# Small-head attention: value products in two runs of six chunks, and stationary operands padded to 128 columns

## The reference, cut to what matters

```python
# L0: 16 heads, head size 8, masked; L3: the same without bias and mask, scale 128 ** -0.5
qh = (q @ Wq.T + bq).reshape(B, 56, 16, 8).transpose(0, 2, 1, 3)      # B = 16
kh = (k @ Wk.T + bk).reshape(B, 1500, 16, 8).transpose(0, 2, 1, 3)
vh = (v @ Wv.T + bv).reshape(B, 1500, 16, 8).transpose(0, 2, 1, 3)
score = einsum('bhqd,bhkd->bhqk', qh, kh) / sqrt(8)
score = where(kv_mask[:, None, None, :], score, -10000.0)
attn = softmax(score, axis=-1)
out = einsum('bhqk,bhkd->bhqd', attn, vh)
return out.transpose(0, 2, 1, 3).reshape(B, 56, 128) @ Wo.T + bo
```

## Time and profile before

| what | value |
|---|---|
| runs, median (lowest, highest) | 2214.21 (2211.83, 2214.41) us |
| span of the profiled execution | 2210.2 us |
| busy in that span: PE, DVE, ACT, POOL | 93%, 67%, 54%, 34% |
| mean granted TensorE clock | 0.953 of 2.4 GHz |
| largest groups of L0: exp L654, reduction L798, product L511 | 198.1, 153.4, 133.5 us |

### The profile page before, as it was taken

The page is one execution under the profiler, slowest core; times in us unless marked ns, Lnnn a source line. Parts: engine busy times, 40 slices in busy tenths (PEclk is TensorE's granted clock), DMA queues, the critical chain, the costliest instruction groups (busy, mean ns, idle before and its releaser), DMA issues. The chain is left out here.

```text
span 2210.2 us, 47308 instructions
## 1 busy us (share of the span) xinstructions
PE 2062.2 (93%) x18797; PEld 1505.9 (68%) x18797; DVE 1482.6 (67%) x3068; ACT 1200.2 (54%) x2313; POOL 752.7 (34%) x337
## 2 busy tenths in 40 slices
PE   5999999866999899999999999999997799999996
PEld 3677777655887455677777777777764457777774
DVE  5677777688986554566666666666626577777774
ACT  5877887634766222344444444444421467777763
POOL 6565566016875470112111211112000254433410
PEclk8999999967999898999999999999997889999997
DMA  6554544233540311231112211131000354544420
GB/s 161 148 148 132 159 134 132 63 85 97 143 136 20 79 38 39 70 104 66 60 60 82 97 60 60 60 100 62 1 1 25 87 159 126 149 126 139 122 79 9
DMA packets 94541, 199.78 MB, mean 90 GB/s; under 512 B 42113, under 2 KB 50353, under 8 KB 94066
## 3 DMA queue, kind: packets, MB, share of 16 engines
q1 hardware_dynamic: 94322, 196.75, 30.3%
HBM read 116.22 MB, written 0.65 MB: 53 GB/s over the span
## 5 line engine op out<-in xcount | busy, mean ns | idle before, releaser
L1630 PEld LDWEIGHTS L2ps<-L2probsT,L2values 125*128 125x128 f32 (+1 forms) x2688 | 317.4, 192 | 51.3 <-issue 48.9
L1611 PE MATMUL L2ps<-L2keys,L2qz 128*128 128x501 f32 x672 | 340.2, 590 | 0.9 <-DVE L2out_bias L1847 0.9
L1630 PE MATMUL L2ps<-L2probsT,L2values 125*128 125x128 f32 (+1 forms) x2688 | 318.5, 275 | 0.5 <-ACT L2probsT L1740 0.5
L1725 POOL TENSOR_TENSOR L2keys<-L2keys,L2mean_spread 127x1500 f32<-127x1500 f32 x15 | 50.9, 3395 | 583.0 <-DMA L2wqk<-L_moments 583.0
L1823 DVE CUSTOM_DVE_ANT_0 L2work<-L2ps,L2maskadd,L2big 128x1503 f32<-128x1503 f32 x112 | 199.5, 1781 | 72.9 <-PE L2ps L1611 72.7
L1625 PEld LDWEIGHTS L2ps<-const,L2work 128*126 128x126 f32 x1344 | 164.3, 140 | 118.7 <-issue 116.5
L654 ACT ACTIVATE L3probsT<-L3ps 128x448 f32<-128x448 f32 x384 | 196.0, 547 | 71.1 <-PE L3ps L511 66.5
L654 ACT ACTIVATE L0probsT<-L0ps 128x448 f32<-128x448 f32 x384 | 198.1, 551 | 47.7 <-PE L0ps L511 46.6
L1625 PE MATMUL L2ps<-const,L2work 128*126 128x128 f32 x1344 | 202.8, 273 | 3.5 <-DVE L2work L1832 3.1
L1742 ACT COPY L2qz<-L2ps 128x128 f32<-128x128 f32 x112 | 29.7, 265 | 304.7 <-PE L2ps L1630 304.7
L798 DVE TENSOR_REDUCE L0partmax<-L0ps 112x1 f32<-112x1000 f32 x128 | 153.4, 1199 | 58.1 <-PE L0ps L484 56.0
(11 more groups left out here) (479 smaller groups left out, 4164.7 us busy)
## 6 DMA issues: line engine op xcount, KB each, us to landing
L0key_stack<-L0key_parts SPq DMA_DIRECT2D x192, 187.5 KB
L3key_stack<-L3key_parts SPq DMA_DIRECT2D x192, 187.5 KB
L0ctxT<-in_ctxT SPq DMA_DIRECT2D x16, 750.0 KB, 4.4
L1rawT<-in_ctxT SPq DMA_DIRECT2D x16, 750.0 KB, 6.5
L2raw<-in_ctx SPq DMA_DIRECT2D x16, 750.0 KB
L3ctxT<-in_ctxT SPq DMA_DIRECT2D x16, 750.0 KB, 4.4
L2mean_spread<-L_moments SPq DMA_DIRECT2D x15, 750.0 KB, 6.7
L2wqk<-L_moments SPq DMA_DIRECT2D x15, 750.0 KB, 8.4
```

The lines of the kernel that those rows point to most:

```text
L1611: last = nc.tensor.matmul(PS[:, 3 * (m % 2) + c, 0:NPR], tile_rows(m), KT[:, m // RT % 2, 500 * c:500 * c + NPR], start=True, stop=True)
L1630: last = nc.tensor.matmul(PS[:, bank, 0:P], V[0:keys_in(c), i // RT % 2, c, :], PT[0:keys_in(c), i % 2, c, :], start=c == 0, stop=c == NCH ...
```

## The change

- `values` is called at two steps of four, n % 4 == 1 and 3, and computes six chunks each time. The waits on `pv_done` and on the emptied S units are counted accordingly.
- QS gets 128 columns per pair, of which the last 16 are zero; `scores0` and `scores12` load all 128 as stationary columns and write all 128 partitions of banks 0 to 2. DVE still reads 112 partitions.
- HL becomes a view of HLW, which has 128 more columns of zeros; M loads 128 stationary columns, from the maxima of its pair on, and writes 128 partitions; ACT still reads the first 2 or 3.
- GpSimd sets the padding to zero at the start, with a semaphore `pads_set`, for which TensorE waits ahead of its loop and DVE ahead of the first `row_maxima`.

```diff
@@ attention_16_small_heads
+    RUNS = 2
+    RUN_STEPS = (1, 3)
...
-        QS = sb("query_stack", [ROWS, 4, 4, TT], BF16)
+        QS = sb("query_stack", [ROWS, 4, 4, P], BF16)
...
-        HL = sb("maxparts", [TT, 2, 4, 2 + NM], BF16)
+        HLW = sb("maxparts", [TT, 2, 4 * (2 + NM) + P], BF16)
+        HL = HLW[:, :, 0:4 * (2 + NM)].rearrange("p u (t n) -> p u t n", t=4)
...
-                    sp.dma_start(QS[n:16 * NC:NC, slot], QM[rows, part, b].rearrange("p j q -> p (j q)")
+                    sp.dma_start(QS[n:16 * NC:NC, slot, :, 0:TT], QM[rows, part, b].rearrange("p j q -> p (j q)")
...
-                nc.tensor.matmul(PS[0:TT, 0, 0:500], QS[0:SROWS, h % 4, tau, :], KS[0:SROWS, h % 4, tau, 0:500],
+                nc.tensor.matmul(PS[:, 0, 0:500], QS[0:SROWS, h % 4, tau, :], KS[0:SROWS, h % 4, tau, 0:500],
...
-                    last = nc.tensor.matmul(PS[0:TT, c, 0:500], QS[0:SROWS, h % 4, tau, :],
+                    last = nc.tensor.matmul(PS[:, c, 0:500], QS[0:SROWS, h % 4, tau, :],
...
             def values(h, part):
                 b, u = divmod(h, 2)
-                wait_emptied(pe, plan.emptied("S", 4 * h + 3, (3 * part + 2) // 4))
+                length = KC // RUNS
+                wait_emptied(pe, plan.emptied("S", 4 * h + 3, (length * (part + 1) - 1) // 4))
...
-                for c in range(3 * part, 3 * part + 3):
+                for c in range(length * part, length * (part + 1)):
...
-                                                QS[:, h % 4, tau, :], start=True, stop=True)
+                                                QS[:, h % 4, tau, 0:TT], start=True, stop=True)
...
-                        last = nc.tensor.matmul(PS[0:2 + NM, bank, tau * TT:(tau + 1) * TT], HL[:, i % 2, tau, :], IB[:],
+                        last = nc.tensor.matmul(PS[:, bank, tau * TT:(tau + 1) * TT], HLW[:, i % 2, tau * (2 + NM):tau * (2 + NM) + P], IB[:],
...
+            pe.wait_ge(s.pads_set, 2)
...
-                h, part = n // 4 - 1, n % 4
-                if 0 <= h < HB:
-                    values(h, part)
+                h = n // 4 - 1
+                if 0 <= h < HB and n % 4 in RUN_STEPS:
+                    values(h, RUN_STEPS.index(n % 4))
...
             nc.gpsimd.memset(MINUS[:], -1.0).then_inc(s.minus_set, 1)
             pool.wait_ge(s.minus_set, 1)
+            nc.gpsimd.memset(QS[:, :, :, TT:P], 0.0).then_inc(s.pads_set, 1)
+            nc.gpsimd.memset(HLW[:], 0.0).then_inc(s.pads_set, 1)
+            pool.wait_ge(s.pads_set, 2)
             if masked:
-                nc.gpsimd.memset(QS[96:97], 125.0).then_inc(s.q_rows_set, 1)
+                nc.gpsimd.memset(QS[96:97, :, :, 0:TT], 125.0).then_inc(s.q_rows_set, 1)
...
-                        act.wait_ge(s.pv_done, 4 * h - 4)
+                        act.wait_ge(s.pv_done, RUNS * (h - 1))
...
-                        act.wait_ge(s.pv_done, 8 * i - 8)
+                        act.wait_ge(s.pv_done, 2 * RUNS * (i - 1))
...
-                    ins = nc.scalar.copy(QS[96:ROWS, i % 4].rearrange("p t n -> p (t n)"), PS[0:2 + NM, bank, 0:HALF])
+                    ins = nc.scalar.copy(QS[96:ROWS, i % 4, :, 0:TT], PS[0:2 + NM, bank, 0:HALF].rearrange("p (t n) -> p t n", t=4))
...
-                act.wait_ge(s.pv_done, 4 * h + 4)
+                act.wait_ge(s.pv_done, RUNS * (h + 1))
...
             def row_maxima(h):
+                if h == 0:
+                    dve.wait_ge(s.pads_set, 2)
```

More of the change, by code:

```diff
@@ L327, in attention_16_small_heads @@
         PS = ctx.enter_context(nc.psum_tensor(name + "ps", [P, 8, BANK], F32))
-        s = semaphores(ctx, nc, name, LN_SEMS + " w_loaded w_ready wv_ready perm_ready bias_ready ones_ready dup_set minus_set rows_set q_rows_set "
+        s = semaphores(ctx, nc, name, LN_SEMS + " w_loaded w_ready wv_ready perm_ready bias_ready ones_ready dup_set minus_set rows_set pads_set q_rows_set "
                        "ctx_loaded0 ctx_loaded1 ctx_loaded2 mask_loaded0 mask_loaded1 stacked0 stacked1 stacked2 stacked3 "
```

## The result

The changed kernel takes 2220.55 us (median of 7 runs, 2215.06 to 2221.80) against 2213.79 for the kernel before in the same session (7 runs): ratio 1.0035 [1.0020, 1.0049]. A second session gave 1.0027 [1.0014, 1.0041]. So it is slower by about 0.3%, just over the 0.2% that the prediction called measurable. The range (2202 to 2225) holds it; the forecast "no change" does not.

A forecast was written before the change was run, and what follows sets the result against it. It took TensorE's in-order queue as the bound, with DVE's reduction closing a loop. Per attention -1.4 steady, +1.3 batches 13 and 14, -0.1 start and end, +0.05 GpSimd; -0.4 for both gave 2214 us, 8-in-10 range 2202 to 2225.

The forecast's parts named there:

- The queue alone: TensorE's queue in a steady batch: 1.8 us less, 24.49 to 22.7, before counting any new waits.
- Rival B: TensorE's queue alone decides and the new waits are not there: 2160 us; chance 0.05.
- The floor of 1.89 at t7-0 and t1-2: Score-product pairs of steps 7 to 0 and 1 to 2: DVE's reduction stops these intervals at 1.89 us.
- The long run: Probability-product run in TensorE's queue: 24 more instructions (three chunks) cost 0.56 us, bounds 0.54 to 0.60.
- M's wait: Maxima unit (L524) waiting for DVE's maxima: 0.34 us at t=2, 0.04 at t=6.
- Rival C: The reduction's floor holds but the maxima unit does not wait: 0.4 us less per batch, 2205; chance 0.13.
- The sum of a batch: Steady batch, its eight pair-to-pair intervals added: 24.36 us against 24.49, a gain of 0.13.
- Batches 13 and 14: Two batches without a K unit: t3-4 hits the floor as well; 22.4 us against 21.8, 0.6 slower each.
- Start and end: First two batches and last one: together -0.1 us per attention, bounds -0.6 and +0.5; last run about -0.3.
- rival E: PE clock at the 1.2 GHz level for a tenth of the loops: some +60 us, 2270; chance 0.03.
- rival D: ScalarE's copy of the sums waits for the longer run, delaying exps in masked attention: 13 us, 2227; chance 0.15.
- A: The forecast itself: the reduction's round trip takes the runs' place; 2214 us, bounds 2208 to 2222; chance 0.64.

## Why the prediction was right in the mechanism and wrong in the sign

By its own steps, with the second profile of the change (span 2215.6), which has no mishap, against the one before (2210.2): 5.4 us more, where 0.4 less was predicted.

1. *The queue alone would save 1.8 a batch.* Right as a price of the queue: with the reduction shortened the batch was 23.37, of which two waits of 0.13 for it (a pair starts 0.33 behind its group, not 0.20) and one of 0.38 for the maxima are left. Without them that is 22.7, as predicted. Rival B (0.05), that these waits are not there, is out.
2. *The floor of 1.89 at t7-0 and t1-2.* Right, both intervals to the hundredth, and right in its cause (short reduction: 0.52 less for 0.53 less of L806).
3. *The long run.* 1.29 from its start to the pair (median of 44 in the second attention; 1890.96 to 1892.26 in the lines above), where the short one had 0.71 (1886.21 to 1886.92): 0.58 for three more chunks, not 0.56. It stood inside the bounds (0.54 to 0.60); choosing near the lower end cost 0.02 four times a batch.
4. *M's wait.* Predicted 0.34 at t=2 from 0.29 to 0.38; measured 0.57 - 0.20 = 0.37, near the upper bound: L819 ended 0.92 after L806 and M started 0.14 later. At t=6 it was 0.08 for 0.04. Rival C, that M does not wait, is out.
5. *The sum of a batch.* This step failed by its size: 0.13 less was predicted (24.36) and nothing measured (24.48 or 24.49). The four long intervals are each 0.04 over the prediction, two light ones 0.02 under it. The 0.04 is 0.02 of step 3 and 0.01 to 0.02 of the pair, which gives way after 0.43 at t=0, 2, 4 and 6, where 0.05 was taken off 0.46. (At t=0 and 2 it comes behind a wait, for which the prediction's own rule takes off 0.03.) The longer waits of step 4 add little, as M and the key product behind it (0.19 and 0.90 at t=2) took about as much less than assumed. Over 22 steady batches it is 2.9 us.
6. *Batches 13 and 14.* 22.4 predicted, 22.61 measured, 21.84 before: 0.77 more each instead of 0.6, mostly the same terms: 0.5 us more over both attentions.
7. *Start and end.* This step failed, in its path and not only in its size. It was put at -0.1 per attention with bounds of -0.6 and +0.5; the last run alone was to bring -0.3. From the last pair to the start of the attention's last instruction the time went from 18.2 to 18.9 in the first and from 18.5 to 20.2 in the second (19.1 and 19.3 in the first profile of the change): 0.7 to 0.9 more, and 1.7 once, of which about 1 is the clock's (step 9). With the padding alone it was 18.2 in all four cases, so it comes with the long runs. The last half batch shows why (kernel before, then kernel after, TensorE):

```profile
2148.88 0.63 PE L484 MATMUL L3ps<-L3key_stack,L3query_stack 96*112 96x500 bf16 x2
...
2150.04 0.78 PE L498 MATMUL L3ps<-L3probsT,L3values 128*32 128x112 f32 x24
...
2151.82 0.36 PE L524 MATMUL L3ps<-L3ident_bf,L3maxparts 112*2 112x112 bf16 x4 [0.70 <-ACT L3probsT L654]
```

```profile
2157.87 0.60 PE L487 MATMUL L3ps<-L3key_stack,L3query_stack 96*128 96x500 bf16 x2
2158.30 0.95 PE L515 MATMUL L3ps<-L3query_stack,L3key_stack 98*128 98x112 bf16 x16
2160.77 0.36 PE L528 MATMUL L3ps<-L3ident_bf,L3maxparts 112*128 112x112 bf16 x4 [1.51 <-DVE L3maxparts L819]
...
2161.45 1.36 PE L502 MATMUL L3ps<-L3probsT,L3values 128*32 128x112 f32 x48
```

   Before, a run of three chunks stood between the last pair and M; M came 2.94 behind the pair then and 2.90 now, so that run had been free. Now those chunks stand behind M, where nothing hides them: 0.19 each by step 3, some 0.6. The prediction counted fewer switches and not where the work went. The start of the first attention was 0.9 longer (30.3 to 31.2, the first pair), and the batches between differ by +0.3 and -1.3 once 13 and 14 are taken off. Of these only the end is explained; starts with their context and weight transfers vary between executions of one kernel too (first pair at 27.8 and at 26.1 after the second attention's start in the two profiles of the change). In all, start, end and first batches are 1.9 and 0.5 longer where -0.1 each was forecast: 2.6 us. Measured, the ends alone are 2.4 (0.7 and 1.7); the starts and the batches between add up to nothing over both attentions, and why they moved each by itself stays open.
8. *GpSimd.* The two memsets took 0.32 and 0.33 and used up the 0.62 of idle time before L121. Priced at 0 to 0.1, and padding alone (first pair of the second attention after 25.9 and 26.1 us in its two profiles, 26.0 before) shows no cost.
9. *The clock.* Between 110 and 165 us it was granted at 1.00, the 2.4 GHz level, through all the waits of the floor; rival E's long loss is out. The rule of the Trainium skill named there (TensorE: Matmul & The Clock Gate, section A second HAM failure mode) is not borne out in these batches: PE waits twice a batch for PSUM banks and the level holds. The clock did cost something at one place that rival E didn't name, the long wait of M in the last half batch. In the second profile of the change PE sat idle there for 1.5 us, the clock was then granted at the 1.2 GHz level for 3.4 us, and the run of six chunks took 2.47 instead of 1.36; in the first profile the same wait left it at 1.00.

```profile
2155.71 0.36 PE L528 MATMUL L3ps<-L3ident_bf,L3maxparts 112*128 112x112 bf16 x4 [1.51 <-DVE L3maxparts L819]
...
2156.39 2.47 PE L502 MATMUL L3ps<-L3probsT,L3values 128*32 128x112 f32 x48
```

```profile
2156.40:2159.80 3.40, 3.40 (x62) 3.07 (x61) 0.00 (x0) 1.87 (x5) 0.00 (x0) 0.50 0.02 5
```

10. *ScalarE (rival D).* Not in this change: idle time before S put down to the exps is 1.1 us in the second attention, 3.9 before, and 5.9 in the masked one, 6.9 before; the batch is 24.48 in the one and 24.49 in the other.

Steps 5 to 7 add up: 2.9 + 0.5 + 2.6 = 6.0 more than the forecast's -0.4, so 5.6. (The forecast's own terms give -0.15 per attention; -0.4 for both comes of rounding twice.) From the start of the first instruction to that of the last, the two attentions took 433.5 and 424.9 against 430.0 and 422.9, 5.5 more. So the mechanism was right, and terms that erred the same way tipped a near zero over the line. The steady batch was put at -0.13 and is 0.00: the added chunks near the lower end of their bounds, and 0.05 off pairs that lost 0.03 to 0.04. The ends were put at -0.3 for the last run and are +0.7 or more, as they were not walked through. Giving only 0.04 of A's chance to "slower" was too sure for a batch at -0.13 with bounds of -0.26 and +0.36.

The larger omission is in the reading, not in the sum: the prediction priced the two halves of the change together. By its own terms (0.03 a pair, 0.30 and 0.20 for M) the padding without the longer runs is 0.7 a batch, and 0.59 was measured.

## What to carry to other kernels

Work that stands between two uses of a buffer held once is not free to remove or to move: take the round trip's length first (here product, 1.20 of reduction, 0.06 back: 1.89), and then ask of every interval whether what is left in it is longer. Spread filler work so that each interval is just over the floor, and check in the same way that its inputs are there at the new place: moved to the right interval, the runs waited for ScalarE instead, and the best order was another in each of two stages that are equal but for the mask. Price the parts of a change apart, as one half can be the whole gain, and walk through the last iteration by itself.

## What the runs showed of the hardware that was not expected

- A product with a stationary operand of only 2 or 3 columns costs more than one of 128: with zeros up to 128, M's four products lost about 0.1 on entering and 0.1 on leaving, 0.37 a batch in all (2211.22 to 2201.93). The partitions written went from 2 or 3 to 128 with it, and the two were not tested apart. The run of 32-column products shows a like cost at both ends, some 0.2 together: between padding alone and the changed kernel, a step that loses its run of three chunks is 0.81 shorter (2.95 to 2.14) and one whose run grows by three is 0.58 longer (4.06 to 4.64).
- Padding a bf16 stationary operand from 112 to 128 columns made its load 99 ns instead of 131, and each pair behind a run or a wait 0.03 to 0.04 shorter. The Trainium skill (TensorE: Matmul & The Clock Gate, section Weight-path perf modes) says that the fast load is on when the number of weights is 128 and the type is not FP32; the trace agrees (98 to 99 ns against 131 to 133).
- One mask transfer for which ACT waited 3.6 us cost the batch 4.6: PE was idle for 1.7 up to 231.2, and from 230.6 on, within that idle time, the clock was granted at the 1.2 GHz level for 6.8 us before it rose again.
